# A macaron block on one core: half of the mixture-of-experts chunks moved from dense evaluation to gathered expert tiles

## The reference

```python
x = x + 0.5 * ffn(layernorm(x))      # first feed-forward
x = x + attention(layernorm(x))      # 16 heads of 64, causal, per sequence of 256 rows
x = x + 0.5 * ffn(layernorm(x))      # the same weights again
# ffn: 64 experts of hidden width 64, and one shared expert
scores = sigmoid(x @ gate_w.T)                       # 64 per row
# 4 of 8 groups of experts by their two best (scores + bias), then the 8 best experts in them
tw = scores of the 8, divided by their sum, * 2.5
y  = sum over the 64 experts e of  w_dense[:, e] * ((silu(x @ wg_e) * (x @ wu_e)) @ wd_e)
y += (silu(x @ sg) * (x @ su)) @ sd
```

## Time and profile before

| | us |
|---|---|
| median of 3 runs | 1830.09 (1829.4 to 1832.41) |
| the profiled execution, its own time | 1831.43 |
| its span, first to last instruction | 1829.7 |
| PE busy | 1781.7 (97%) |
| DVE busy | 1331.9 (73%) |
| ACT busy | 774.6 (42%) |
| POOL busy | 36.6 (2%) |
| transfers | 149.60 MB, 36.9% of 16 DMA engines |

### The profile page before, as it was taken

How to read it: one execution, slowest core, us unless ns; L and a number is a source line. 1 busy time by engine, 2 the same in 40 slices (tenths; PEclk the granted TensorE clock), 3 DMA queues, 4 the chain that set the end, 5 groups by cost and what they waited for, 6 DMA issues and landing times.

```text
span 1829.7 us, 30208 instructions
## 1 busy us (share of the span) xinstructions
PE 1781.7 (97%) x9049; PEld 1255.0 (69%) x9049; DVE 1331.9 (73%) x3327; ACT 774.6 (42%) x1971; POOL 36.6 (2%) x84
## 2 busy tenths in 40 slices
PE   5899999999999999999999999879999999999999
PEld 3566666666666667777778777756666666666665
DVE  5777677676776678888888888767677676777765
ACT  3333323233232256767666666633323233232322
POOL 0000000000000000000000000000000000000000
PEclk8999999999999999999999999999999999999999
DMA  9954554455545500000000000034554455544553
GB/s 206 173 122 110 115 117 105 107 115 115 117 100 109 116 1 2 0 0 0 0 0 0 0 0 0 1 82 109 120 118 108 107 122 121 117 104 111 120 124 75
DMA packets 109530, 149.60 MB, mean 82 GB/s; under 512 B 30128, under 2 KB 43056, under 8 KB 109488
## 3 DMA queue, kind: packets, MB, share of 16 engines
q1 hardware_dynamic: 109488, 149.08, 36.9%
HBM read 144.87 MB, written 4.19 MB: 81 GB/s over the span
## 4 chain that ended last, share of the span: by engine, by line
PE 61%; DVE 2%; DMA 0%; issue 0%; ACT 0%; SPq 0%; POOLq 0%; POOL 0%; DVEq 0%
PE banks L521 12%; PE banks L489 7%; PE banks L487 7%; PE banks L488 7%; PE banks L1059 6%; PE banks L1099 5%; PE banks L1080 4%; PE banks L1116 3%; PE banks L1024 2%; PE banks L1063 2%; PE banks L1025 2%; PE banks L1026 2%; PE banks L1043 1%; PE banks L1044 1%; PE banks L1042 1%; DMA f_mix_wide<-mix_rows 0%
## 5 line engine op out<-in xcount | busy, mean ns | idle before, releaser
L592 ACT ACTIVATE f_hid<-banks 128x512 f32<-128x512 f32 x528 | 315.4, 597 | 835.9 <-PE banks L521 831.5
L648 DVE TENSOR_TENSOR f_hid<-banks,f_hid 128x512 f32<-128x512 f32 x528 | 363.9, 690 | 338.0 <-ACT f_hid L592 336.3
L521 PE MATMUL banks<-f_hid,wd 128*128 128x512 f32 x1056 | 540.7, 594 | 10.7 <-DVE f_hid L659 10.6
L487 PE MATMUL banks<-r_xT_hi,wg_hi 128*128 (+1 forms) x528 | 393.0, 744 | 2.4 <-PEq L951 2.4
L659 DVE TENSOR_TENSOR f_hid<-f_mix_wide,f_hid 128x512 f32<-128x512 f32 x512 | 352.9, 690 | 38.4 <-DMA f_mix_wide<-mix_rows 24.3
L521 PEld LDWEIGHTS banks<-f_hid,wd 128*128 128x128 f32 x1056 | 196.8, 188 | 67.6 <-DVE f_hid L659 13.1
L487 PE MATMUL banks<-r_xT_hi,wu_hi 128*128 (+1 forms) x528 | 209.9, 398 | 0.0
L489 PE MATMUL banks<-r_xT_lo,wu_hi 128*128 (+1 forms) x528 | 209.9, 398 | 0.0
L488 PE MATMUL banks<-r_xT_hi,wu_lo 128*128 (+1 forms) x528 | 208.8, 396 | 0.0
L489 PE MATMUL banks<-r_xT_lo,wg_hi 128*128 (+1 forms) x528 | 208.3, 394 | 0.0
L488 PE MATMUL banks<-r_xT_hi,wg_lo 128*128 (+1 forms) x528 | 207.3, 393 | 0.0
(11 more groups left out here) (153 smaller groups left out, 2155.4 us busy)
## 6 DMA issues: line engine op xcount, KB each, us to landing
f_mix_wide<-mix_rows SPq DMA_DIRECT2D x252, 512.0 KB, 6.5
landing<-in_L_ffn_We_gate SPq DMA_DIRECT2D x4, 512.0 KB, 7.1
landing<-in_L_ffn_We_up SPq DMA_DIRECT2D x4, 512.0 KB, 7.8
wd<-in_L_ffn_We_down SPq DMA_DIRECT2D x4, 512.0 KB, 6.8
mix_rows<-r_mixT SPq DMA_DIRECT2D x32, 64.0 KB, 2.1
out<-x_all SPq DMA_DIRECT2D x8, 256.0 KB, 6.7
f_mix_wide<-mix_rows SPq DMA_DIRECT2D x4, 384.0 KB, 5.4
f_mix_wide<-mix_rows SPq DMA_DIRECT2D x4, 128.0 KB, 3.0
```

Of the source, the lines that this page charges most:

```text
L487: nc.tensor.matmul(bank[:, :], hi, rhs_hi, start=start, stop=False)
L521: nc.tensor.matmul(acc[:, :], w["wd"][:, p * P:(p + 1) * P], hid[:, p % HIDS, :], start=(p == 0), stop=(p == PAIRS)).then_inc(down_done, 1)
L592: nc.scalar.activation(hid[:, p % HIDS, :], gate_bank[p % 3][:, :], ACT.Silu).then_inc(silu_done, 1)
L648: nc.vector.tensor_tensor(hid[:, p % HIDS, :], up_bank[p % 3][:, :], hid[:, p % HIDS, :], ALU.mult)\
```

## The change

Everything in the feed-forward is written anew; in attention the extra work is laid between the steps.

- **Dense half.** In each `ffn` 4 of 8 chunks stay dense: chunks 0 to 3 in the first (`FIRST`), 4 to 7 in the second (`SECOND`). Gate and up products are one plain fp32 matmul each instead of three fp32r ones; hi/lo copies of the weights are gone, and with them room for all weights in one copy (`gu`, `wd`).
- **Sparse half.** The other 4 chunks (2048 rows, 8 experts each, 16384 pairs of row and expert) are routed by 23 steps of `route`, which leave a mask; `count`, `plan`, `rank` and `place` give every pair a row number in a list ordered by expert, each expert's part rounded up to tiles of 128. `dispatch` scatters the normalised rows to `x_rows` in DRAM with 128 indirect transfers from POOL. `quads` then runs over the list, four tiles at once. A tile belongs to one expert, whose number is read into a PE register. The length of the list is fixed at compile time for the worst case: (16384 - 64) // 128 + 64 = 191 tiles, 48 quads; before them come 4 quads with the shared expert (`j < SPARSE`). The results go to `y_rows` in DRAM. `weigh` makes the 8 weights of each row; the combiner gathers 8 rows for each row by 128 more indirect transfers (`gather`) and adds them with their weights (`add`, 8 a tile, each waiting for the last).
- **Order.** First `ffn`: 132 dense slots, with the routing among them, then 52 quads. Attention, now unrolled: the first ffn's `gather` and `add` in steps 0 to 22, the second's routing from step 6 to 48, its `dispatch` from step 49. Second `ffn`: routing of its first dense chunk alone, 33 dense slots, 52 quads, 99 dense slots with `gather` and `add` among them.
- **Queues.** The expert and attention weights are now issued by ACT, as are three transfers that clear `x_rows` (24576 x 128 numbers, 12.6 MB), all ahead of its slot 3. `copy_q` moves from DVE to ACT.

The core of the diff; the numbers of lines are not shown. First the order of the chunks and the dense slot:

```diff
+TILES = (TOPK * SPARSE * CHUNK - E) // P + E
+QUADS_R = -(-TILES // CT)
...
+FIRST = routes_of([(0, True), (1, True), (4, False), (5, False), (6, False), (7, False), (2, True), (3, True)])
+SECOND = routes_of([(0, False), (1, False), (2, False), (3, False), (4, True), (5, True), (6, True), (7, True)],
+                   by_row=SPARSE)
...
-                three(g, "wg", p, xh, xl).then_inc(gate_done, 1)
...
-                three(u, "wu", p, xh, xl).then_inc(up_done, 1)
...
+            nc.tensor.matmul(gate_bank[g % 3][0:rows, :], w["gu"][:, 0, experts, :].rearrange("p e f -> p (e f)"), x,
+                             start=True, stop=True).then_inc(gate_done, 1)
...
+            nc.tensor.matmul(up_bank[g % 3][0:rows, :], w["gu"][:, 1, experts, :].rearrange("p e f -> p (e f)"), x,
+                             start=True, stop=True).then_inc(up_done, 1)
```

The indirect transfers, and the quad on PE, DVE and SP:

```diff
+        def dispatch(k, t):
...
+            for j in range(TOPK):
+                nc.gpsimd.indirect_dma_start(
+                    x_rows[:, :], bass.IndirectOffsetOnAxis(ap=b.idx[:, f, CT * k + t, j:j + 1], axis=0),
+                    b.xk[:, k, t, :], None).then_inc(scattered, 16)
...
+        def turn(j):
...
+            if j >= SPARSE:
+                i = j - SPARSE
+                pe.wait_ge(loaded[i % 3], 16 * (i // 3 + 1))
...
+            for t in range(CT):
+                src = b.xk[:, j, t, :] if j < SPARSE else q.xq[:, (j - SPARSE) % 3, t, :]
+                mm = nc.tensor.transpose(A[j % 2][:, t * P:(t + 1) * P], src, w["ident"][:, :])
...
+            _, expert[j] = nc.values_load_multi_w_load_instructions(
+                b.ids[i:i + 1, :], engines=PE_ONLY, min_val=0, max_val=E,
...
+        def gate_up(j):
+            load_experts(j)
...
+            for t in range(CT):
...
+                mm = nc.tensor.matmul(B[j % 2][:, t * P:(t + 1) * P], q.xqT[:, j % 2, t * P:(t + 1) * P], wt,
+                                      start=True, stop=True)
...
+        def step(j):
+            if ok(j):
+                turn(j)
+            if ok(j - 1):
+                gate_up(j - 1)
+            if ok(j - 2):
+                turn_hid(j - 2)
+            if ok(j - 3):
+                down(j - 3)
...
+        def take_y(j):
+            dve.wait_ge(y_done, j + 1)
...
+            nc.vector.tensor_copy(q.yq[:, i % 2, :, :].rearrange("p t d -> p (t d)"), ends[j % 2][:, :])\
+                .then_inc(y_read, 1)
...
+        def load(i):
...
+            if i >= 3:
+                sp.wait_ge(turned, SPARSE + i - 2)
+            sp.dma_start(q.xq[:, i % 3, :, :], rows(x_rows, i)).then_inc(loaded[i % 3], 16)
+
+        def store(i):
+            sp.wait_ge(y_read, SPARSE + i + 1)
+            sp.dma_start(rows(y_rows, i), q.yq[:, i % 2, :, :]).then_inc(y_stored[i % 2], 16)
+
+        def step(i):
+            if i < QUADS_R:
+                load(i)
+            if i >= 3:
+                store(i - 3)
```

ACT's order at the start of the first `ffn`:

```diff
+            load_weights(0)
+            act.wait_ge(gw_turned, 1)
+            nc.scalar.copy(w["gw"][:, :], acc[:, 0:E]).then_inc(gw_copied, 1)
+            copy_xT(FIRST[0])
+            load_weights(1)
+            sigmoid(FIRST[0])
+            for g in range(3):
+                slot(g)
+            copy_mixT(FIRST[0])
+            load_weights(2)
+            load_weights(3)
+            load_others()
+            clear_rows()
+            for g in range(3, NS + 5):
+                slot(g)
```

## The result

The changed kernel takes 2659.18 us, median of 4 runs (2652.92 to 2663.42), against 1830.43 for the kernel before beside it (4 runs): 1.4517 times as long, 95% interval 1.4496 to 1.4538. The profiled execution has a span of 2660.4 us. The direction was as predicted; the time lies 329 us above the forecast and 99 above the range.

A forecast was written before the change was run, and what follows sets the result against it. PE's work was taken to bound the kernel. Less dense work left 1307.4 us; quads 864, shared quads and drains 38, start 50, second head 19, more drains 16, DVE 12, attention 25, less 1.3, gave 2330 us; range 2070 to 2560.

The forecast's parts named there:

- Quads: Sparse halves of both feed-forwards: 96 routed quads at 9.0 us each, +864 us, with PE idle for some 4.9 at full clock.
- the terms from down's end to the load's landing: Within a quad: take_y 0.9 us, store issue 0.45, load to landing 3.4, waking PE 0.1.
- its own part: PE's 22 pairs in a quad: 2.5 us at full clock, taken as 3.7 because the clock falls in pauses.
- registers: Reading four expert numbers on PE each quad: 0.5 us; rival of 2 us or more, total 2570, chance 0.08.
- loads run ahead: Rival in the quads: SP's wait doesn't delay loads, so 2.8 us a quad, total 1736 us, faster; chance 0.08.
- Dense slots, shared quads, drains: Feed-forwards: 264 dense slots at 2.56 us, +82; 8 shared-expert quads at 2.7, +22; fills and drains, +16 and +16.
- The start: First feed-forward: ACT's issues of weights and zeros delay slot 3 to about 85 us; +50, ends +10 and +80.
- Attention: Steps of 9.11 us, DVE busy 7.5, gain chained adds and routing, lose copy_q: +25 us, ends 0 and +60.
- POOL's transfers: Rival: POOL's 512 indirect transfers bind at 2.5 us each, +140, +120 and +100, total 2690 us; chance 0.12.
- the limits of 1.4 and 1.5: Microseconds per indirect transfer hidden on POOL: 1.4 in the first feed-forward, 1.5 in attention's gathers; 1.15 in the dispatch.
- the ring: Quads: SP's order chains down, take_y, store, next load and PE's turn, so nothing is hidden; 7.85 us at full clock.
- The first-byte figure: POOL's indirect transfers: about 1 us to the first byte, by which all three sets would be hidden at no cost.

The follow-up runs named there:

- the kernel with full clock: The changed kernel with SP's stores issued five quads back instead of three: 2088.19 us.
- group 5 and 6: Two occasions of one kernel, the changed one with stores five quads back and fixed experts instead of register loads: 1848.98 us, then 2090.60 us.
- the kernel with the ring mended: The changed kernel with stores five quads back instead of three: 2088.19 us, repeated at 2092.13; with fixed experts too, 1848.98 and 2090.60.
- plain_transfers_on_pool: The changed kernel with its 512 indirect transfers replaced by plain ones of 128 contiguous rows at the same places: 2362.88 us.
- repaired_spread: The changed kernel with stores five back, weights on POOL, scatters in landed groups, attention's adds split and spread: 1784.19 us, ratio 0.9741 to the kernel before.
- groups 2 and 6: Kernels run together on one chip: single transfers in the old kernel (1880.58, 1831.77), start issues on POOL (2064.55); later two repeats (2092.13, 2090.60).
- group 3: Kernels run together: the old kernel with transfers landed in pairs (1834.16) or fours (1832.48), and the changed kernel with all found causes removed (1970.81).

## Why the prediction was right or wrong

- **Quads.** Right in mechanism: 8.8 us against 9.0, 20 us less over 96. That the size is so near is in part luck: PE stood 4.27 us a quad where the terms from down's end to the load's landing gave 4.85 (landing 3.1 instead of 3.4), and its own part took about 4.5 where 3.7 and 0.5 for registers had been put. A granted clock of 0.56 over the quads means nearly the lower level throughout (the prediction's bounds were 4.2 if it falls every time and 5.0 if it never recovers); the registers cost 0 in the kernel with full clock. The loop that the Trainium skill, "TensorE: Matmul & The Clock Gate", section on HAM oscillation, describes as throttled in every turn is what the stretch at 0.56 shows, and it is gone in the stretch at 1.00 once the loads ran ahead. The 200 ns a register that the Trainium skill, "Runtime: NRT & Kernel Launch", section Instruction fetch mechanics, gives are seen in no run: four numbers a quad add nothing to a period of 2.83 us. The rival "loads run ahead" had its price right as well, 2.8 a quad, once its condition was made true.
- **Dense slots, shared quads, drains.** Nothing to correct in the sum: where neither pauses nor the start disturb, the plain slot takes 2.58 (2.56).
- **The start.** Mechanism right, 92 instead of 85. The sum behind the 85 was slack: 22.6 MB less 8.4 MB at 213 to 286 GB/s, and 15 us, give 65 to 82.
- **Attention: the step that failed.** Priced +25 us with ends 0 and +60; its copies of y are 794.7 us apart instead of 514.5, +280. Two errors of different kinds are in it. First, 71 us are its own added work. I took the two rows for 48 steps apart, but the copies between them come every 33.65 us, so they are 13 sequences, 52 steps: a step took 8.41 us and not 9.11. DVE's share of it leaves 1.5 us and not 1.6, so the free time itself was hardly mis-sized. Mis-sized was how much of it eight adds in one piece at a step's end can use: spread, attention took 561, 47 more than before, with 208 transfers in it.
- **POOL's transfers: the rival whose price was taken at the wrong place.** I asked how long a transfer occupies POOL (0.96 busy, 1.27 apart, under the limits of 1.4 and 1.5 that the prediction gave, a little over 1.15) and concluded by these limits; the effect on the other engines stood at nothing. What they cost is the other engines' time, 210 us in attention. That the rival's 2690 lies near the measured 2659 is luck: it stood on 2.5 us of POOL for each transfer, where the changed kernel has 1.27. The pair of group 5 and 6 puts it at 2091 - 1849 = 242 us for the kernel with the ring mended: 48 in the first dense half (first shared quad at 523 instead of 475), 202 in attention, 16 in the last slots, some 19 between quads and attention, less some 42, since without pauses attention ends before POOL's scatters do and the second feed-forward then waits for POOL. In the changed kernel it is as much within a few per cent (attention 794.7, first quad 525). Taken off, 2659 would be about 2415, an estimate: 85 above the forecast, inside the range. Why the pauses come at all is open.
- **The first-byte figure** of the Trainium skill, "DMA: Bandwidth & Descriptors", section Latency and other measured facts (about 1 us), was no guide: no run shows the first byte, issue to landing took 2.2, and neither is what cost.

By stage, the 329 us are about 80 before the first quad (59 of it pauses, against `plain_transfers_on_pool`), -20 in the quads, +255 in attention, of which 210 are pauses, and +16 in the last slots; the rounded terms come to 331.

## What to carry to other kernels

A queue's order is a dependency like any other: a load queued behind a store's wait made 96 quads three times as long, and a distance of five instead of three removed 571 us. When an engine gets a new kind of instruction, ask not only whether it has the time, but what the instruction does to those beside it; 24 transfers in a loop of the old kernel would have told, on an occasion with the pauses. Where rows of them can't be avoided, four at a time with a wait for landing was the cheapest form that still kept up: `repaired_spread`, with that and its adds spread, is the one version that beats the kernel before. And before a term is divided by a count of steps, the count is to be read from rows in between.

## What the runs showed of the hardware that I had not expected

- Indirect transfers of POOL, issued 1.27 us apart, can hold the waiting instructions of PE, ACT and DVE: about 1.0 to 1.1 us for each in rows of 12 and more, 0.8 in rows of 8, an estimated 0.1 to 0.2 in fours, nothing one at a time (2.51 apart). Under dense slots it was less: 0.4 in rows of 32, 0.12 in eights. Plain transfers of POOL, 0.53 us apart, don't.
- This is not always so: the same kernel took 1848.98 and 2090.60 us on different occasions, and one chip had the pauses in groups 2 and 6 and not in group 3. What decides it is open. So is whether the recording has a part in it: the traces with pauses lack semaphore events, and all times shown here come with a recorded span, so none compares with an execution that was not recorded. The period of the quads doesn't hang on it: in `plain_transfers_on_pool`, which has no pauses, the turns are 8.78 us apart too.
- A clear of 128x1024 on POOL (0.97 us) costs attention 0.4 us, though POOL itself had time.
- Moving issues off ACT gave half of what was expected at the start: with half of the weights, the attention weights and the clearing issued by POOL, slot 3 came 25 us earlier, not 50; one issue that was left on ACT grew from 5 to 24 us.
